# Starting both dense feed-forwards of a four-layer kernel with group 0: transposes, router products and lower halves moved into the attentions

## The reference

```python
x = x + _L0_xattn_ref(ctx_1024, ctx_1024, _layernorm(x), mask, W_out, b_out)   # 16 heads
x = x + _L0_ffn_ref(_layernorm(x), W1, b1, W2, b2, Wr, br)    # 8 experts, hidden 512
x = x + _L1_xattn_ref(_layernorm(x), ctx_1024, W_q, b_q, W_k, b_k, W_v, b_v)   # one head
x = x + _L1_ffn_ref(_layernorm(x), ...)                       # 8 experts + 1 shared, hidden 256
...                                                           # L2 and L3: heads and sparse experts

# a dense feed-forward, in short
logits  = x @ Wr + br
weights = softmax or top-2 softmax of the logits, zero for the other experts
h       = gelu(einsum('td,edh->teh', x, W1) + b1)
out     = einsum('ted,te->td', einsum('teh,ehd->ted', h, W2) + b2, weights)
```

## Time and profile before

| | |
|---|---|
| runs, median (lowest, highest) | 1169.02 us (1167.01, 1169.91) |
| the profiled execution: own time, span | 1170.76 us, 1169.0 us |
| busy over the span | TensorE 960.7 (82%), VectorE 621.5 (53%), ScalarE 556.4 (48%), GpSimd 393.3 (34%) |
| L2229, L2230, L2231, hidden products of both dense feed-forwards | 86.4, 80.2 and 80.2 us, 200 matmuls each |
| L2243, their output products | 119.4 and 70.1 us |
| L2283, gelu | 136.7 us in 200 |
| first hidden product of L0f and of L1f | at 127.20 and 380.71 us |

### The profile page before, as it was taken

The page is one execution under the profiler, slowest core; times in us unless marked ns, Lnnn a source line. Parts: engine busy times, 40 slices in busy tenths (PEclk is TensorE's granted clock), DMA queues, the critical chain, the costliest instruction groups (busy, mean ns, idle before and its releaser), DMA issues. The chain is left out here.

```text
span 1169.0 us, 20619 instructions
## 1 busy us (share of the span) xinstructions
PE 960.7 (82%) x7766; PEld 808.3 (69%) x7766; DVE 621.5 (53%) x1703; ACT 556.4 (48%) x1069; POOL 393.3 (34%) x386
## 2 busy tenths in 40 slices
PE   4888899999997999978898874889377876299992
PEld 3666789999976899955665654889245554288882
DVE  7885421111145443377878765345398775444443
ACT  2665444444435434445666550665345543155552
POOL 4443200100013101410101345356465557545552
PEclk9999899999997999998989895899779986599997
DMA  9999900000000000000000001766200001445543
GB/s 349 189 189 188 205 1 1 2 1 1 1 1 1 1 1 1 1 1 1 2 2 2 19 20 50 229 189 206 81 1 2 1 1 41 146 145 168 172 151 108
DMA packets 70577, 83.83 MB, mean 72 GB/s; under 512 B 5297, under 2 KB 57528, under 8 KB 70352
## 3 DMA queue, kind: packets, MB, share of 16 engines
q1 hardware_dynamic: 64336, 71.98, 25.5%
q0 software_dynamic: 4992, 8.45, 2.1%
q10 hardware_dynamic: 1152, 2.10, 0.5%
HBM read 52.15 MB, written 32.18 MB: 72 GB/s over the span
## 5 line engine op out<-in xcount | busy, mean ns | idle before, releaser
L2283 ACT ACTIVATE hT<-PS,par 128x512 f32<-128x512 f32 x200 | 136.7, 688 | 179.2 <-PE PS L2231 177.6
L2323 DVE SCALAR_TENSOR_TENSOR X<-PS,wts,X 128x128 f32<-128x128 f32 x272 | 76.6, 344 | 226.4 <-PE PS L2243 226.3
L1092 ACT ACTIVATE hT<-PS 116x512 f32<-116x512 f32 (+1 forms) x192 | 102.0, 561 | 103.7 <-PE PS L865 102.4
L865 PE MATMUL PS<-par,score 128*116 128x128 f32 x704 | 109.7, 293 | 24.7 <-DVE oc L996 12.9
L2243 PEld LDWEIGHTS PS<-regA,hT 128*128 128x128 f32 x1024 | 119.2, 192 | 2.8
L2243 PE MATMUL PS<-regA,hT 128*128 128x128 f32 x1024 | 119.4, 275 | 0.0
L865 PEld LDWEIGHTS PS<-par,score 128*116 128x116 f32 x704 | 81.0, 143 | 42.2 <-issue 31.7
L1162 POOL TENSOR_TENSOR score<-score,mx 128x1232 f32<-128x1232 f32 x32 | 72.0, 2251 | 91.1 <-DVE mx L976 91.1
L1997 PE MATMUL PS<-q_up,halves 128*112 128x256 f32 (+1 forms) x276 | 85.6, 310 | 8.8 <-DVE hT L2106 8.8
L2229 PE MATMUL PS<-x_up,w_halves 128*128 128x512 f32 x200 | 86.4, 432 | 0.0
L1069 ACT ACTIVATE score<-score 128x1232 f32<-128x1232 f32 x64 | 78.3, 1223 | 11.8 <-POOL score L1162 9.5
(11 more groups left out here) (313 smaller groups left out, 2021.3 us busy)
## 6 DMA issues: line engine op xcount, KB each, us to landing
regA<-L3f_w SPq DMA_DIRECT2D x23, 704.0 KB, 4.1
regB<-L2f_w SPq DMA_DIRECT2D x23, 578.0 KB, 4.1
L2f_sorted_x<-empty_row SPq DMA_DIRECT2D x8, 1161.0 KB, 20.0
L3f_sorted_x<-empty_row SPq DMA_DIRECT2D x8, 1161.0 KB, 19.5
regA<-L0f_w SPq DMA_DIRECT2D x4, 768.0 KB, 16.9
regA<-L2f_sorted_x SPq DMA_DIRECT2D x23, 129.0 KB, 3.7
regB<-L3f_sorted_x SPq DMA_DIRECT2D x23, 129.0 KB, 4.0
par<-params SPq DMA_DIRECT2D x1, 2450.0 KB, 13.9
```

The costliest lines, as they stand in the source:

```text
L865: last = nc.tensor.transpose(PS[0:BW, bank_of(("exps", 3 * u + i)), (j % 4) * P:(j % 4) * P + P], exps_of(u)[:, first:first + BW], ident)
L1092: nc.scalar.activation(hT[0:BW, u % 2, i, 0:width], PS[0:BW, bank, 0:width], ACT.Copy).then_inc(pT_ready.sem, 1)
L2283: nc.scalar.activation(hT[:, n % 2, k, :], PS[:, i % 4, :], c["act"], bias=pc(f"{tag}_b1")[:, col:col + 1]).then_inc(h_ready.sem, 1)
```

## The change

In L0x the transposes of the next norm's groups 0, 1 and 2 go to the ends of iterations 8, 12 and 16, in the round of banks 4 and 5, their router products to iterations 9, 13 and 17, into the free end of bank 6, and ScalarE's evacuations behind the exponentials. GpSimd makes x_low of groups 0 and 1 behind shifts 12 and 15, of group 2 behind the first weights' halves. In L1x group 0 is transposed after block 2, group 1 and the router product of group 0 after block 3, all through bank 7. L0f begins with hidden(0), transposes of group 3, hidden(1), router product of group 3; L1f with group 2, hidden(0), group 3, hidden(1), each with a router product behind. ScalarE does the exp of the router after the gelus of hidden(1). In L1f VectorE applies the norm to group 3 in place of ScalarE. No arithmetic is added or removed.

```diff
@@ norm_stage
             def transpose_group(pe, g, at=None):
-                pe.wait_ge(xn_ready.sem, xn_ready.at(TG * (g + 1)))
+                if on_scalar and g == NG - 1:
+                    pe.wait_ge(xn_last.sem, xn_last.at(TG))
+                else:
+                    pe.wait_ge(xn_ready.sem, xn_ready.at(TG * (g + 1)))
...
             def scalar(a, st):
                 for g in range(NG):
-                    if on_scalar and g == NG - 1:
-                        scalar_apply(a, g)
                     scalar_group(a, g)
+
+            def scalar_rest(a, st):
+                for g in (1, 2):
+                    scalar_group(a, g, 7)
@@ attention_stage
+            next_group_at, next_logits_at, next_lower_at = ({8: 0, 12: 1, 16: 2}, {9: 0, 13: 1, 17: 2}, {12: 0, 15: 1}) if tag == "L0x" else ({}, {}, {})
...
                     if 0 < u <= units:
                         sums_back(u - 1)
+                    if u in next_logits_at:
+                        after_nm["route_tensor"](pe, next_logits_at[u])
                     if done is not None:
                         out_transpose(done)
...
+                    if u in next_group_at:
+                        n = next_group_at[u]
+                        wait_for_bank(pe, ("next", n))
+                        after_nm["transpose_group"](pe, n, bank_of(("next", n)))
@@ attention_stage, scalar, end of iteration u
+                    if u in next_group_at:
+                        after_nm["scalar_group"](a, next_group_at[u], bank_of(("next", next_group_at[u])))
@@ attention_stage, pool, after shift t
+                    if t in next_lower_at:
+                        after_nm["lower"](p, next_lower_at[t])
@@ single_stage
+                    if b == 2:
+                        after_nm["transpose_group"](pe, 0, 7)
+                    if b == 3:
+                        pe.wait_ge(after_nm["upper_ready"].sem, after_nm["upper_ready"].at(1))
+                        after_nm["transpose_group"](pe, 1, 7)
+                        after_nm["route_tensor"](pe, 0)
...
+                    if b == 3:
+                        after_nm["scalar_group"](a, 0, 7)
                     if b:
                         after_nm["scalar_apply"](a, b - 1)
@@ ffn_stage, tensor
-                nm["tensor"](pe, ro["tensor"])
-                pe.wait_ge(upper_ready.sem, upper_ready.at(NG))
-                hidden(0)
-                ro["tensor_counts"](pe)
+                elif tag == "L0f":
+                    hidden(0)
+                    next_transposes(3, 5)
+                    hidden(1)
+                    ro["tensor"](pe, 3)
+                    pe.wait_ge(upper_ready.sem, upper_ready.at(NG))
+                else:
+                    next_transposes(2, 7)
+                    ro["tensor"](pe, 1)
+                    hidden(0)
+                    next_transposes(3, 7)
+                    ro["tensor"](pe, 2)
+                    hidden(1)
+                    ro["tensor"](pe, 3)
+                    pe.wait_ge(upper_ready.sem, upper_ready.at(NG))
                 for n in range(steps):
-                    if n + 1 < steps:
+                    if n + 1 < steps and not (ahead and n == 0):
                         hidden(n + 1)
                     output(n)
@@ ffn_stage, scalar
+                    if ahead and n == 1 and k == 0:
+                        nm["scalar_group"](a, 3, {"L0f": 5, "L1f": 7}[tag])
+                    if ahead and n == 2 and k == 0:
+                        ro["scalar"](a, st)
@@ ffn_stage, GpSimd
             def pool_early(p, st):
                 split_weights(p, st, 0)
+                if groups_lowered:
+                    lower(p, groups_lowered - 1)
```

More of the change, by code:

```diff
@@ L830, in wait_for_bank @@
                 free = {"exps": pT_ready, "rows": route and route["rows_read"], "logits": route and route["logits_read"],
-                        "ranks": route and route["ranks_read"], "back": o_used, "own": own and own["read"], "q": own and own["q_used"]}[kind]
+                        "ranks": route and route["ranks_read"], "back": o_used, "own": own and own["read"], "q": own and own["q_used"],
+                        "next": after_nm.get("upper_ready")}[kind]
                 pe.wait_ge(free.sem, free.at(n + 1))
@@ L1297, in tensor @@
             def tensor(pe, g):
+                if tag == "L0f" and g == 0:
+                    pe.wait_ge(par_in_2, 16)
                 pe.wait_ge(xT_ready.sem, xT_ready.at(g + 1))
                 for t in range(TG * g, TG * g + TG):
[L1301 removed]
+                    last = nc.tensor.matmul(logits_space[:, t * E:t * E + E], xnT[:, t * P:t * P + P], pc(f"{tag}_wr"),
                                             start=True, stop=True)
@@ L2195, in ffn_stage @@
             upper_ready, logits_read, x_first = nm["upper_ready"], ro["logits"], ro["x_first"]
+            ahead = tag in ("L0f", "L1f",)
+            groups_lowered = {"L0f": 3, "L1f": 1}[tag] if ahead else 0
             c = FFNS[tag]
@@ L2551, in build @@
                 ff = ffn_stage(tag, nm, ro, kv, norm_after_ffn)
+                next_norm.update(route_tensor=ro["tensor"], lower=ff["lower"])
                 add(dict(pool=ff["pool_early"]))
-                add({k: nm[k] for k in ("vector", "scalar", "pool")})
+                if tag in ("L0f", "L1f",):
+                    add(dict(vector=nm["vector"], scalar=nm["scalar_rest"] if tag == "L1f" else None, pool=nm["pool"]))
+                else:
+                    add({k: nm[k] for k in ("vector", "scalar", "pool")})
             else:
```

42 lines of the change are left out of this document (28 added, 14 removed).

## The result

The change came out faster, but by much less than forecast: 1165.65 us median of 20 runs (1158.01 to 1169.40) against 1168.14 of 20 runs of the kernel before (1165.12 to 1172.28), a ratio of 0.997 with an interval of 0.9956 to 0.9984. The profiled execution took 1165.65 us, its span is 1163.9 at a mean granted clock of 0.912. So 2.5 us were won by the medians, where 9.0 were forecast. The two profiled executions lie further apart, 1169.0 against 1163.9, because the one of before was 2.6 us over its own median (1170.76 against 1168.14).

A forecast was written before the change was run, and what follows sets the result against it. TensorE bounds the feed-forwards, so their dense stretches should start earlier: 1169.0 - 5.9 (L0) - 3.0 (L1) = 1160.1 us, 1160.0 against the median. Range 1156.5 to 1165.5 us.

The forecast's parts named there:

- The place of the bound: Inside a feed-forward only TensorE counts; time is won only by starting its dense stretch earlier or keeping holes out.
- Rival E: L0f does not start earlier, since hidden(0) still waits for its x_low behind the last group's work; chance 0.03.
- L0x's cost, 2.4 plus 1.2: In L0x, groups 0 and 1 cost 2.4 us together, and group 2 delays the last out-transpose by 1.2.
- The bound from below, 1.9: Least cost of groups 0 and 1 in L0x: four transposes and four products, 0.5 us each, twice.
- Rival C: Attention pays 2.8 us or more per group through bank waits and GpSimd meeting VectorE; 1163 to 1166 us; chance 0.10.
- L0f's start: First b2 transposes of L0f come 8.3 us earlier, less 2.4 spent in L0x: gain 5.9, TensorE assumed at 2.4 GHz.
- Rival A: L0f's 1.2 us idle lowers TensorE's clock, hidden(0) at half speed; 2 of 5.9 gone; 1162 to 1164 us; chance 0.14.
- L1f's start, 3.0: First b2 transposes of L1f start at 387.6 instead of 390.55, gain 3.0 us, after a new 2 us stall.
- group 0's transposes go into the third block, where TensorE waits anyway: In L1x, group 0's transposes fall into existing TensorE waiting; no cost was counted.
- Downstream ... each feed-forward runs as before: After two outputs and the start of the b2 transposes, L0f and L1f each run unchanged.
- the 0.15 left out of the range: Chance outside 1156.5 to 1165.5 us: worse half of three rivals and what later stages add by their clock.
- Rivals D and F: D: clock falls at two idle places, stays low, 1178 us, 0.03; F: attention's slow stretches shrink, 1157 to 1158 us, 0.10.

The follow-up runs named there:

- e6: Kernel before plus six idle matmuls per block of L1x, results unused; 1166.87 us, ratio 0.9976 to the kernel before.
- The cut kernel: Whole change, ended behind L1f without layers 2 and 3, or its L0 part alone ended there: 505.59 and 505.83 us; kernel before ended there 512.74.
- the cut kernels: Kernel before, whole change, L0 part and L1f part, each ended behind L1f without layers 2 and 3: 512.74, 505.59, 505.83 and 510.96 us.
- e10: Whole change with L0x router products moved: groups 0 and 1 behind later scores, group 2 behind the last projection; 1183.58 us, ratio 0.9973 to the kernel before.
- the cut change: Whole change ended behind L1f without layers 2 and 3; 505.59 us (4 runs), against 512.74 for the kernel before ended there too.
- e5: Whole change plus six idle matmuls per block of L1x, results unused; 1162.85 us, ratio 0.9944 to the kernel before.
- e9: L0 part alone (L1f as before) with L0x router products moved into waits and behind the last projection; 1185.03 us, ratio 0.9976 to the kernel before.
- e2: L0 part of the change alone, L1x and L1f as in the kernel before; 1161.85 us, ratio 0.9934 to the kernel before.

## Why the forecast was wrong, step by step

- **The place of the bound** was right for L0f. Starting its dense stretch earlier won time: hidden(0) of L0f starts right behind the last projection, on average at 122.5 (nine traces) instead of 128.8 (five): 6.3 earlier, forecast 6.6. It was not the only thing that wins: e6 starts nothing earlier and times 2.6 us less. Rival E did not occur.
- **L0x's cost, 2.4 plus 1.2.** The last out-transpose is 3.9 later by the means of nine and five traces, against 3.6. The router products were mis-sized: 0.5 where 1.06 is right, in three groups, and once more for group 3. The bound from below, 1.9, was thereby too low as well. By that the delay should have been 1.7 us over the forecast's 3.6, and it was 0.3 over. One wait for VectorE is 0.4 shorter (1.01 at 84.29 for 1.41); what made up for the rest is not shown. That the sum came out so near is luck. Rival C did not occur.
- **L0f's start.** Hidden(0) took 4.45 instead of 2.9, since the clock fell as it began (121.8), behind idle moments between the last projections; I had assumed 2.4 GHz. Rival A was about right in its size (it had the transposes of group 3 at 1.2 later than forecast, they stand 1.4 later) and wrong in its cause: the idle of 1.2 that was to bring it did not exist, because the slow hidden(0) covered the apply. B2 came 5.0 earlier by the means of all traces (141.28 against 146.24), forecast 5.9. The terms are about these: the later start of hidden(0) (0.3), its low clock less the idle that did not come (0.3), and the products of group 3 at twice their price (0.5). The cut kernel gained 6.9, more than the traces account for.
- **L1f's start, 3.0.** Right from the last outputs on (20.98 against 24.09 by the means of the six and six traces listed, and a stall of 2.04 for the forecast 2). Wrong in "group 0's transposes go into the third block, where TensorE waits anyway": they stand ahead of the wait and cost 0.85. That makes 2.2.
- **The sum up to here** is 7.2, and the cut kernels show 7.15. The parts do not agree as well (L0 5.0 by the traces and 6.9 cut, L1f on top of it 2.2 and 0.2), so the agreement is in part chance.
- **The steps that failed.** Two terms were too large: L0f's start, by 0.9 (a clock assumed full, products at half their length), and L1f's, by 0.8 (transposes taken as free that cost 0.85). That is 1.7 of the 5 to 6.5 us that are missing. The rest falls on "Downstream ... each feed-forward runs as before", and with it on carrying 1169.0 - 5.9 - 3.0 over to the whole kernel. What the runs show in its place: behind L1f's first b2 the same code takes 772.7 to 778.6 us, and one stretch in it 167.6 to 172.7 by where TensorE's clock falls. The cut kernels put 3 to 4.7 us there, with the uncertainty above. The cause of this part stays open. I had put "what later stages add by their clock" into the 0.15 left out of the range; it is as large as the effect.
- **The yardstick.** The trace that the sum was made on was 2.6 us above the later median of its kernel; such a pair of traces shows twice the gain of the medians (5.1 against 2.5).
- **Rivals D and F** did not occur. The kernel is not slower, and in the trace after the clock stayed full behind the 2.04 us stall in L1f; the gain is smaller than forecast, not larger.
- **Table loads.** The trace has gelu's load at 123.34 for 1.28 and the activation at 124.63, and exp's load at 130.35 right at the end of the gelu before it. The Trainium skill, in ScalarE: Activation LUTs, section What ACT_TABLE_LOAD costs, adds a drain of about 1380 ns; by it the exp of L0f would have been 1.4 behind its load. The trace has it 0.3 behind, and those 0.3 are a wait for VectorE.

## What to carry to other kernels

Count a moved step by the records of one group of it and not by a share of a row: here a float32 matmul leaves two records and a transpose one. A place "where the engine waits anyway" is one behind the wait's start and ahead of its end; look which instruction bears the idle time in brackets, and put the work directly ahead of that one. Even then the gain has to reach the end: e10 shortened the wait and not the kernel. Where untouched stages idle a lot, time the touched ones alone too, cut behind them, and with more than 4 runs: the cut change spread over 4.5 us, most of what it won.

## What the runs showed of the hardware

- TensorE stayed at its 1.2 GHz level for some 27 us (about 351 to 378) while it was busy 4.3 to 5.0 of every 5 us, and from 364 to 378 without a pause that the trace shows. Its last idle moments before the fall were 2.49 us (up to 341.04), 0.90 and 0.68 (up to 348.90). With six extra matmuls per block (e5) it was at 2.4 GHz through all of L1x.
- The same kernel took 1168 us on some chips and 1187 on two others, with a mean granted clock of 0.898 in e9 against 0.909 in e2, both with the L0 part. At L2x's first scores e9 was not behind (517.5 against 521.2); L2x alone took 170.0 us in e9 and 161.6 in e2.
- Four VectorE applies took 1.12 us with GpSimd idle, 2.17 us in L1f beside a GpSimd x_low, and 3.01 beside two.
